# One buffer per tile for turned probabilities, and both tiles' value products in one run

## The reference, cut to what matters

```
attn = softmax(q k^T / 4)           # self: 128 x 128 for each window and each of 16 heads
o    = attn v                       # "values", head size 16
attn = softmax(top16(q kc^T / 4))   # cross: 128 queries x 77 context tokens, 16 heads
o    = attn vc
```

## Time and profile before

| | us |
|---|---|
| three runs | 1450.96, 1445.49, 1446.76 |
| median | 1446.76 |
| span of the profiled execution | 1447.1 |
| PE busy in that span | 1413.0 (98%) |
| DVE busy | 1061.7 (73%) |
| ACT busy | 837.8 (58%) |
| POOL busy | 437.8 (30%) |

### The profile page before, as it was taken

One profiled execution on the slowest core, in us unless ns is written; L12 is line 12 of the kernel. 1 busy time (PEld: TensorE's weight loads), 2 busy tenths in 40 slices (PEclk: granted clock), 3 DMA queues, 4 the chain that ended last, 5 costly groups with the idle time before them and its releaser, 6 DMA issues.

```text
span 1447.1 us, 30246 instructions
## 1 busy us (share of the span) xinstructions
PE 1413.0 (98%) x9777; PEld 1195.1 (83%) x9777; DVE 1061.7 (73%) x4754; ACT 837.8 (58%) x2555; POOL 437.8 (30%) x599
## 2 busy tenths in 40 slices
PE   7999999999999999999999999999999999999997
PEld 5778788888888888888888788888888878887886
DVE  3585869688796878879696777959688786968642
ACT  3464475757566384755757466574757547574433
POOL 1314132333325232332335232233334313232302
PEclk9999999999999999999999999999999999999999
DMA  7520000010000000010010000000010000000000
GB/s 244 196 73 2 1 1 25 1 34 9 19 31 15 1 2 25 2 34 2 21 36 2 15 2 16 11 15 20 8 43 8 16 2 1 9 2 8 1 2 14
DMA packets 27342, 34.99 MB, mean 24 GB/s; under 512 B 3325, under 2 KB 22449, under 8 KB 26930
## 3 DMA queue, kind: packets, MB, share of 16 engines
q1 hardware_dynamic: 27185, 33.07, 7.1%
HBM read 28.83 MB, written 4.22 MB: 23 GB/s over the span
## 4 chain that ended last, share of the span: by engine, by line
PE 83%; DVE 12%; issue 2%; ACT 1%; SPq 0%; POOL 0%; DMA 0%; DVEq 0%; ACTq 0%; POOLq 0%
PE bank L965 13%; PE bank L920 12%; PE bank L989 10%; PE bank L972 7%; PE bank L791 6%; PE bank L929 6%; PE bank L777 4%; PE bank L852 4%; PE bank L840 4%; PE bank L904 4%; DVE knocked L2224 3%; PE bank L830 2%; PE bank L748 2%; PE bank L762 2%; PE bank L812 1%
## 5 line engine op out<-in xcount | busy, mean ns | idle before, releaser
L920 PE MATMUL bank<-hB,Wm 128*128 128x256 f32 x1024 | 242.3, 383 | 2.2 <-ACT hB L1366 2.2
L920 PEld LDWEIGHTS bank<-hB,Wm 128*128 128x128 f32 x1024 | 190.6, 190 | 33.4 <-issue 7.0
L965 PE MATMUL bank<-nxT,W1nx 128*128 128x256 f32 x896 | 212.1, 382 | 0.0
L1405 ACT ACTIVATE prob<-bank,rmax 128x128 f32<-128x128 f32 x512 | 180.3, 432 | 28.3 <-DVE rmax L2151 28.3
L1762 POOL TENSOR_TENSOR scores<-scores,M 128x308 f32<-128x308 f32 x128 | 94.5, 738 | 320.1 <-DVE knocked L2224 317.7
L1412 ACT ACTIVATE probT<-bank 128x512 f32<-128x512 f32 (+1 forms) x256 | 140.3, 617 | 83.8 <-PE bank L904 76.8
L989 PE MATMUL bank<-W2p,gT 128*128 128x256 f32 x768 | 183.2, 381 | 3.0 <-DVE acc L2303 1.9
L965 PEld LDWEIGHTS bank<-nxT,W1nx 128*128 128x128 f32 x896 | 166.1, 191 | 23.1 <-issue 2.8
L989 PEld LDWEIGHTS bank<-W2p,gT 128*128 128x128 f32 x768 | 141.2, 190 | 23.8 <-issue 2.8
L1450 ACT ACTIVATE tbs<-bank,b1half 128x256 f32<-128x256 f32 x128 | 60.7, 474 | 143.1 <-PE bank L920 102.2
L1466 ACT ACTIVATE tbs<-bank,betaH 128x256 f32<-128x256 f32 x224 | 95.6, 489 | 82.7 <-PE bank L972 82.7
(11 more groups left out here) (238 smaller groups left out, 2772.4 us busy)
## 6 DMA issues: line engine op xcount, KB each, us to landing
Wm_g<-in_L_xcond_w_m_dram SPq DMA_DIRECT2D x4, 1024.0 KB, 5.4
W1ev<-in_L_xcond_e_w_dram SPq DMA_DIRECT2D x6, 512.0 KB, 7.2
x<-in_x_dram SPq DMA_DIRECT2D x16, 128.0 KB, 2.6
x<-in_x_dram SPq DMA_DIRECT2D x32, 64.0 KB, 2.3
Wm<-in_L_xcond_w_m_dram SPq DMA_DIRECT2D x1, 2048.0 KB, 9.3
out_dram<-acc SPq DMA_DIRECT2D x16, 128.0 KB, 1.7
out_dram<-acc SPq DMA_DIRECT2D x32, 64.0 KB, 2.0
batch_rows<-row_store SPq DMA_DIRECT2D x4, 384.0 KB, 3.9
```

The source lines that it names most:

```text
L920: m = pe.matmul(bank_of(name)[:, half * UT:(half + 1) * UT], Wm1[:, k, c:c + P], hB[:, k, :], start=(k == 0), stop=(k == CB - 1))
L965: pe.matmul(bank_of(name)[:, n * UT:(n + 1) * UT], W1nx[:, k, c0 + n * P:c0 + (n + 1) * P], nxT[:, k, :], start=(n == 0 and k == 0), stop= ...
L1405: m = act.activation(prob[:, s, i, :], psum[s][:, i * P:(i + 1) * P], ACT.Exp, bias=rmax[:, t, s * HPS + i:s * HPS + i + 1], accum_out=rsu ...
```

## The change

`probT` gets a dimension for the tile. In the 14 passes tile 0's value products move down PE's list, to stand directly ahead of tile 1's: for cross attention past `b_turn_weights`, the first-layer products, `a_turn_picked(1, ...)` and `b_router`; for self attention past `b_second(1, ...)`, `b_first_nx("h21")`, `a_turn_probs(1, ...)`, the evidence products and `a_turn_inverses("r1")`. `last_cross` has the same edit for cross attention. The prologue's order stays. The lists of DVE, ACT, POOL and SP are not touched. Room for the second buffer comes from three small tiles of the prologue: `out_row` and `onehot` now lie in tiles that the passes write first (`bias_term`, `bias_sum`), and `split_b` shrinks.

```
-        probT = sb("probT", [P, SLOTS, HPS, P])
+        probT = sb("probT", [P, TILES, SLOTS, HPS, P])
...
-        out_row = sb("out_row", [1, C])
+        out_row = bias_term[0:1, 0, :]
...
-        split_b = sb("split_b", [NB, 4, C], BF16)
-        onehot = sb("onehot", [NB, NB, P])
+        split_b = sb("split_b", [1, len(SHARED), C], BF16)
+        onehot = bias_sum[0:NB, :, :].rearrange("b t c -> b (t c)").rearrange("b (n q) -> b n q", q=P)
...
-                                          v[:, f * SLOTS + s, 32 * e:32 * e + 32], probT[0:np_, s, f * PAR + e, :],
+                                          v[:, f * SLOTS + s, 32 * e:32 * e + 32], probT[0:np_, t, s, f * PAR + e, :],
...
                 b_first_nx("h01", 2 * P, b)
-                if r == 0:
-                    pe.wait_ge(values_read, batch + 1)
-                a_cross_values(0, c)
                 b_turn_weights(b)
...
                 b_router(b)
+                if r == 0:
+                    pe.wait_ge(values_read, batch + 1)
+                a_cross_values(0, c)
                 a_cross_values(1, c)
...
                 a_scores(1, range(SLOTS), a)
-                a_values(0, a)
                 b_second(1, (0, 1), b)
...
                 a_turn_inverses("r1", "pv", a)
+                a_values(0, a)
                 a_values(1, a)
...
-                act.activation(probT[0:np_, s], psum[s][0:np_, :].rearrange("p (i q) -> p i q", i=HPS), ACT.Copy)\
+                act.activation(probT[0:np_, t, s], psum[s][0:np_, :].rearrange("p (i q) -> p i q", i=HPS), ACT.Copy)\
```

More of the change, by code:

```diff
@@ L395, in bass_pixart_experts @@
         gated_loads = [(Wso_g[:, :, :], blocks(w_so)), (Wco_g[:, :, :], blocks(w_co))]
-        folded_loads = [every_batch(rrow[:, :], router_b), (out_row[:, :], rank1(out_b)), (rows[0:1, BIAS.index("g2"), :], rank1(gate_b2)),
+        folded_loads = [every_batch(rrow[:, :], router_b), (out_row, rank1(out_b)), (rows[0:1, BIAS.index("g2"), :], rank1(gate_b2)),
                         (Rw[:, :, :], blocks(router_w)), (outw, blocks(out_w)), (wk_sb, blocks(wk1)), (wq_sb, blocks(wq1))]
@@ L2046, in expert_bias @@
                     r = rows[0:1, BIAS.index("e0") + e, :]
-                    i = dve.scalar_tensor_tensor(r, bk[0:1, (e % 2) * C:(e % 2 + 1) * C], 4.0, out_row[:, :], ALU.mult, ALU.add)
+                    i = dve.scalar_tensor_tensor(r, bk[0:1, (e % 2) * C:(e % 2 + 1) * C], 4.0, out_row, ALU.mult, ALU.add)
                     if e != es[-1]:
```

## The result

The changed kernel takes 1473.13 us (median of four runs, 1470.84 to 1475.08) against 1446.8 for the kernel before: a ratio of 1.0166, with a 95% interval of 1.0148 to 1.0183, or 21.4 to 26.5 us more. The direction and the place were forecast. The size was not: 1473 is above the forecast of 1465 and 2 us above the top of the range.

The account below looks back on a forecast made before the run. PE bounds the kernel (busy 98% of the span, 83% of the last chain). Cross 0.55 plus self 0.76 lose 1.31 a pass, 18.3 over 14 passes; `last_cross` saves 0.2, so +18.1 gives 1465 us, range 1452 to 1471.

Parts of the forecast that it names:

- The runs were cover, and the loss is PE standing where they were: Both attention halves: without tile 0's run PE waits for DVE, 0.79 at `pw`, 0.90 in self attention.
- The price of a merged run: Value runs of both tiles: a second run directly behind the first adds 0.87 us, against 1.01 alone.
- The wait for `pw`: Cross attention, `b_turn_weights`: PE stands still 0.79 us for DVE, so the turn starts only 0.39 earlier, not 1.01.
- The next turn that can wait is the second pair of `a_turn_picked(1, ...)`: Cross attention, behind `pw`: this pair needs DVE's mask, so PE falls from 0.39 to 0.32 us early.
- 0.87 - 0.32 = 0.55: Cross attention, at tile 0's scores: the moved run's price less PE's early arrival, 0.55 us later a pass.
- 0.87 - 0.11 = 0.76: Self attention: the moved run's price less PE's early arrival after the last weighing, 0.76 us later a pass.
- The sum: Whole kernel: 1.31 us lost a pass, 18.3 over 14 passes, less 0.2 saved in `last_cross`: +18.1.
- The second (one wait only): Rival 2: only the cross or only the self wait shows, 1453 or 1454 us; chance 0.10.
- the first (no waits): Rival 1: the merge pays and the waits don't show, 5.5 us gained, 1441 us; chance 0.10.
- The third: Rival 3: each wait costs more than the release, as weights can't be loaded ahead; 1.8 a pass, 1472 us; chance 0.04.
- The upper bound of 1.70 a pass: All passes: each moved run costs 1.01 and neither half finishes early; 23.6 us in all, 1470 us.

Follow-up runs that it names:

- both covered: Changed kernel with other ready PE products (half of h10's first-layer products, evidence products) in the two moved runs' old places; ratio 1.0001 to the kernel before, passes -0.28 us.
- the halves: Changed kernel with only tile 0's cross products, or only its self products, merged and moved: passes +12.11 and +12.09 us, ratios 1.0097 and 1.0107 to the kernel before.

## Why the prediction was right in direction and short in size

- **The runs were cover, and the loss is PE standing where they were: right.** Both waits came at the named lines, in every pass; with cover put back ("both covered") both are gone and so is the loss. That the halves add up was right (12.11 + 12.09).
- **The price of a merged run: right.** 1.88 for the pair is 2 x 0.87 + 0.14. The merge as a whole is worth 0.45 a pass, I had 0.37; the gap is the way into self attention's second run, which I hadn't counted.
- **The wait for `pw`: right.** It was done at 1289.16 + 0.32 = 1289.48, PE began 0.06 later, and stood 0.38 earlier in the pass than before (forecast 0.39). The wait reads 0.60 and not 0.79 because the profile's end of the work ahead is modelled: 1285.28 + 16 x 0.216 = 1288.74, so 0.80 by starts.
- **The step that failed: "The next turn that can wait is the second pair of `a_turn_picked(1, ...)`", and with it 0.87 - 0.32 = 0.55.** The first turn starts 1295.34 - 1285.28 = 10.06 behind the first-layer products, and before 1270.67 - 1260.56 = 10.11: of the 0.38 the bank of the query biases takes 0.33, and POOL's kept inverses take the rest (all of it, where the bank's wait is covered). The cross half loses 0.87, not 0.55: 0.32 x 14 = 4.5 us. I had followed the data that each turn reads, and neither the bank that it writes nor the turn behind it, whose data come from POOL.
- **The same in self attention, smaller: 0.87 - 0.11 = 0.76.** The last weighing ended at 1319.56 + 0.69 = 1320.25 and its turn began at 1320.40 by the chain, 0.15 later, where I had taken the 0.05 of the earlier trace rows. That is all but 0.01 of the 0.11: 1.5 us. The first turn shows the same 0.15 (1316.22 + 0.69 = 1316.91, begun at 1317.06). The earlier trace rows is a wait for masked scores; the kernel before had three waits for the weighing itself, and in the one of pass 8 shown above the turn begins 0.14 after DVE's end at 784.35 + 1.02 = 785.37. With that release the last turn of pass 14 had nothing to spare.
- **The sum.** 18.3 + 4.5 + 1.5 = 24.3 against 24.10 measured in the passes. The other 2.35 of the profiled span lies ahead of pass 1 and is there, or not, with the same prologue.
- **Rivals.** The second (one wait only) and the first (no waits) fell by the profile alone. The third had the right size, some 1.8 a pass and 1472, but its reason doesn't reach so far. The groups behind the waits took 0.28 (L950), 0.47 (the first of L840) and 1.78 (L904), from start to next start, against 0.28, 0.44 and 1.74 before, so what a wait costs beyond the release is 0.04 at most. The release of 0.15 may be a part of what the rival describes, but it accounts for 0.1 of the 0.41 by which a pass was longer than forecast.

The upper bound of 1.70 a pass came close by luck. Its words give PE no credit for being early, which was the case here, but its sum still takes off the 0.32 of the cross half, and it prices each run at 1.01 where 0.87 was paid: the two errors nearly cancel (1.74 with both put right, 2.02 with its words and its price). The rows of before could have shown that there was no credit: the turn of the kept inverses had no time to spare.

## What to carry to other kernels

Before work is moved on an engine that never rests, list every wait between its old and its new place, for data and for the bank that is written, from all engines, each with its spare time: if one of them has none, nothing that is gained ahead of it passes, and the moved work costs its whole length at the new place. Take the time from a result's end to PE's start from a wait for that same result. Then list what waits for the moved instruction, in the same way. A merge that saves 0.2 at each of its places pays only if work that is ready takes over the cover, and then only in the stretches in which no other engine's chain is as long as this one's.

## What was not expected of the hardware

In pass 14 of the changed kernel a turn behind a weighing began 0.15 after DVE's end, both times, and the turn of `pw` 0.06 after it; in each the tile that was waited for is what is loaded as weights (loads of 0.14 in both). The scores that waited for ACT's reading of the inverses' bank began 0.36 after its end. Why these differ stays open. DVE's weighing took 1.02 in place of 0.69 while POOL worked on the next batch's weights. The start of pass 1 varied from 122.0 to 125.6 between kernels with the same prologue work, in step with the granted clock there, which is more than most edits of this study are worth; a difference of spans has to be split by stages before it is put down to an edit.
